# Layer 0's score maxima by half batches, most of them beside the attention that uses them

## The reference, cut to what matters

```python
scores = jnp.einsum('bhqd,bhkd->bhqk', q, k) * scale
scores = jnp.where(causal, scores, -jnp.inf)
y_ar = jnp.einsum('bhqk,bhkd->bhqd', jax.nn.softmax(scores, axis=-1), v)
e = v[:, :, 1:, :] - y_ar[:, :, :-1, :]
...
y_ma = jnp.einsum('bhqk,bhkd->bhqd', ma, e)
```

## Time and profile before

| | us |
|---|---|
| runs | 725.0, 719.17, 721.73 (median 721.73) |
| profiled execution, its own time | 721.84 |
| its span, first to last instruction | 720.0 |
| busy PE, DVE, ACT, POOL | 511.9, 365.3, 196.8, 182.3 |
| reductions of maxima on DVE (L1059), 160 of 690 ns | 110.0 |
| matmuls of maxima without the masks' (L1378, `sb_m_sets`), 160 | 82.5 |
| exps on ACT (L812), 80 of 1,026 ns | 80.3 |
| mean granted TensorE clock | 0.863 |

### The profile page before, as it was taken

How to read it: one execution, slowest core, us unless ns; L and a number is a source line. 1 busy time by engine, 2 the same in 40 slices (tenths; PEclk the granted TensorE clock), 3 DMA queues, 4 the chain that set the end, 5 groups by cost and what they waited for, 6 DMA issues and landing times.

```text
span 720.0 us, 9924 instructions
## 1 busy us (share of the span) xinstructions
PE 511.9 (71%) x3706; PEld 329.5 (46%) x3706; DVE 365.3 (51%) x950; ACT 196.8 (27%) x278; POOL 182.3 (25%) x208
## 2 busy tenths in 40 slices
PE   1755784799899889998878529914778888735930
PEld 1624432344634544453467517802445655524930
DVE  4444745367676856760535431224969677430211
ACT  1342231453245144336234302102223111101200
POOL 8550436001010110111012560045322022031035
PEclk9987887699999999999989958965899999655975
DMA  8434668732442253142070012114743530001213
GB/s 282 185 116 148 210 212 248 177 103 64 92 133 78 79 131 104 53 90 82 1 234 1 30 39 57 45 32 132 203 142 79 160 97 16 1 15 51 60 40 98
DMA packets 61471, 74.16 MB, mean 103 GB/s; under 512 B 6772, under 2 KB 38128, under 8 KB 61168
## 3 DMA queue, kind: packets, MB, share of 16 engines
q1 hardware_dynamic: 59376, 69.34, 33.3%
...
## 4 chain that ended last, share of the span: by engine, by line
PE 47%; DVE 18%; POOL 11%; issue 8%; DMA 6%; ACT 5%; SPq 5%; POOLq 0%; DVEq 0%; ACTq 0%
PE ps_accum L1378 21%; PE ps_pair L1378 16%; PE ps_turn L1378 5%; POOL xe_scr L574 4%; DMA sb_ring<-sb_qs 3%; SPq L358 2%; POOL sb_rstd L558 2%; PE ps_turn L1386 2%; DVE sb_work L1132 2%; POOL sb_work L720 2%; DVE sb_work L1270 1%; DVE sb_mpart L1059 1%; DVE sb_values L969 1%; DVE sb_stats L960 1%; SPq L366 1%
## 5 line engine op out<-in xcount | busy, mean ns | idle before, releaser
L812 ACT ACTIVATE sb_work<-ps_pair 128x1024 f32<-128x1024 f32 x80 | 80.3, 1026 | 51.0 <-PE ps_pair L1378 50.2
L1059 DVE TENSOR_REDUCE sb_mpart<-ps_turn 128x4 f32<-128x512 f32 x80 | 55.0, 687 | 46.6 <-PE ps_turn L1378 46.5
L1378 PE MATMUL ps_pair<-sb_ring,sb_xsets 128*128 128x512 f32 x160 | 64.5, 480 | 15.6 <-DMA sb_ring<-sb_qs 10.1
L1059 DVE TENSOR_REDUCE sb_mpart<-ps_accum 128x4 f32<-128x512 f32 x80 | 55.0, 688 | 20.9 <-PE ps_accum L1378 20.2
L1378 PE MATMUL ps_accum<-sb_work,sb_v_aug 128*32 128x128 f32 (+3 forms) x768 | 58.6, 400 | 0.3 <-ACT sb_work L812 0.3
L1378 PE MATMUL ps_turn<-sb_ring,sb_m_sets 128*128 128x512 f32 x80 | 40.5, 506 | 20.7 <-DMA sb_m_sets<-q_scr 11.0
L1378 PE MATMUL ps_accum<-sb_ring,sb_m_sets 128*128 128x512 f32 x80 | 42.0, 525 | 3.9 <-DVE sb_mpart L1059 3.7
L1378 PEld LDWEIGHTS ps_pair<-sb_ring,sb_xsets 128*128 128x128 f32 x160 | 30.7, 199 | 26.6 <-issue 14.5
L556 POOL TENSOR_SCALAR sb_ve<-sb_mv 128x4 f32<-128x4 f32 x24 | 5.6, 235 | 144.4 <-DVE sb_mv L963 144.0
L624 POOL TENSOR_TENSOR sb_e_pad<-sb_v_next,sb_y_ar 128x128 f32<-128x128 f32 x16 | 7.3, 458 | 127.2 <-DVE sb_y_ar L1102 127.2
L1270 DVE TENSOR_TENSOR sb_work<-ps_pair,sb_cst 128x1024 f32<-128x1024 f32 x32 | 37.5, 1215 | 2.2 <-PE ps_pair L1378 2.2
...
## 6 DMA issues: line engine op xcount, KB each, us to landing
...
```

The costliest lines, as they stand in the source:

```text
L812: act.activation(banks[:, 2 * i:2 * i + 2], pair[u % 2][:], ACT.Exp, scale=SCALE).then_inc(s["exp_done"], 1)
L1059: dve.tensor_reduce(mpart[:, m // NPAIR, m % NPAIR, :], max_banks[m % 2][:].rearrange("p (h k) -> p h k", h=HL), AX.X, ALU.max).then_inc(s ...
L1378: return pe.matmul(dst, lhsT, rhs, start=start, stop=stop, skip_group_check=True)
```

## The change

Maxima are numbered through over all batches (n from 0 to 159), and finished by half batches q (two sets, HALF = 20 units) where they were finished by batches.

- Ahead of attention only batch 0's first 20 units are run: 12 in front 3, none in front 2, eight behind the fronts.
- In attention, batch 0's slot 0 has 20 units (sets 2 and 3 of batch 0 itself), and each slot after it ten: slots 1 to 3 of batch b have the first three sets of batch b+1, slot 0 of batch b+1 its last. So batch 3's slot 0 has ten units, and its other slots none. In slots 1 and 3 a slot's first step has none, and the other four have 3, 2, 3, 2.
- `max_of_tiles`, `max_turn` and `max_t` are done for each half batch: eight times where there were four, once ahead of attention, and then in step u = 5 (half 2b+1) and step u = 15 (half 2b+2) of the first pass. ACT's copy stands behind the exp of that step and behind `answers_out`. `mT` has two tiles of 8 rows. The first unit of a half waits until ACT has copied the half before.
- On SP, set 2 and set 3 of batch 0's maxima are loaded ahead of `keep_features(2)` and `keep_softmax(3)`; `load_exp_set(0, ...)` stands behind `keep_features(3)`; `next_max_set(2)`, which holds until unit 29 has run, stands ahead of `load_state(0)`; a row of maxima is issued right behind its set's loads.

```diff
--- before.py
+++ after.py
@@ -106,6 +106,27 @@
 LAST_OF_UNIT = [EXP_PAIRS[2 * i + 1][0] for i in range(NPAIR // 2)]
 NM, NX, NG_X = NS * NPAIR, NS * NPAIR // 2, NPAIR // 2
 STEPS = NS * NT
+HALF = 2 * NPAIR
+UNITS = B * NS * NPAIR
+
+
+def max_units(b, u):
+    hs, i = u // NG_X, u % NG_X
+    if b == 0 and hs == 0:
+        return HALF + 4 * i, HALF + 4 * i + 2, HALF + 4 * i + 4
+    first = NPAIR * (NS * b + NS - 1 + hs)
+    if first >= UNITS:
+        return UNITS, UNITS, UNITS
+    at = (0, 0, 3, 5, 8, 10) if hs % 2 else (0, 2, 4, 6, 8, 10)
+    return first + at[i], first + (at[i] + at[i + 1]) // 2, first + at[i + 1]
+
+
+def max_turn_in(b, u):
+    if u == NG_X:
+        return 2 * b + 1
+    if u == 3 * NG_X and b + 1 < B:
+        return 2 * b + 2
+    return None
 
 def build(nc, x_in, bias_cols, w_attn_t, w_k2_t, w_proj_t, b_proj, w1_t, w2_t, b2,
...
@@ -387,18 +408,16 @@
                     hold(sp, s["v_aug"], b)
                 sp.dma_start(values_of[b % 2][:], v_scr[b].rearrange("(t p) d -> p t d", p=P)).then_inc(s["v_in"], 16)
-            def next_max_set(b, hs):
-
-                hold(sp, s["smax_mm"], NM * b + NPAIR * (hs + 1))
-                if hs + 2 < NS:
-                    load_max_set(b, hs + 2)
-                elif b + 1 < B:
-                    load_max_set(b + 1, hs + 2 - NS)
+            def next_max_set(n):
+
+                hold(sp, s["smax_mm"], NPAIR * (n + 1))
+                if n + 2 < B * NS:
+                    load_max_set((n + 2) // NS, (n + 2) % NS)
             def max_row(b, hs):
                 sp.dma_start(ring[3 * HD:3 * HD + 1, hs % 2].bitcast(F32),
-                             mT[HL * hs:HL * hs + HL].bitcast(F32)).then_inc(s[f"xset{hs % 2}"], 16)
+                             mT[hs // 2][HL * (hs % 2):HL * (hs % 2) + HL].bitcast(F32)).then_inc(s[f"xset{hs % 2}"], 16)
             def keep_values(b):
@@ -433,45 +452,42 @@
             keep_values(2)
             keep_softmax(1)
             keep_features(1)
-            next_max_set(0, 0)
             keep_values(3)
-            next_max_set(0, 1)
             keep_softmax(2)
+            next_max_set(0)
             keep_features(2)
+            next_max_set(1)
             keep_softmax(3)
+            keep_features(3)
             hold(sp, s["ffn_h"], NF * B)
             for hs in range(2):
                 load_exp_set(0, hs)
-            keep_features(3)
             hold(sp, s["v_kept"], 16 * B)
             load_values(0)
-            for kept in ("q_kept", "k_kept"):
-                hold(sp, s[kept], 48 * B)
-            next_max_set(0, 2)
             hold(sp, s["max_t_evac"], 1)
             for hs in range(2):
                 max_row(0, hs)
-            next_max_set(0, 3)
-            for kept in ("mq_kept", "mk_kept"):
+            for kept in ("q_kept", "k_kept", "mq_kept", "mk_kept"):
                 hold(sp, s[kept], 48 * B)
             hold(sp, s["zeroed"], 7)
             for b in range(B):
+                if b == 0:
+                    next_max_set(2)
                 load_state(b)
                 if b + 1 < B:
                     load_values(b + 1)
                 for hs in range(NS):
-                    if b + 1 < B:
-                        next_max_set(b + 1, hs)
+                    if NS * b + NS - 1 + hs < B * NS:
+                        next_max_set(NS * b + NS - 1 + hs)
                     hold(sp, s["st_mm"], NX * b + NG_X * (hs + 1))
                     if hs + 2 < NS:
                         load_exp_set(b, hs + 2)
+                        hold(sp, s["max_t_evac"], 2 * b + 2)
                         max_row(b, hs + 2)
                     elif b + 1 < B:
                         load_exp_set(b + 1, hs + 2 - NS)
-                if b + 1 < B:
-                    hold(sp, s["max_t_evac"], b + 2)
-                    for hs in range(2):
-                        max_row(b + 1, hs)
+                        hold(sp, s["max_t_evac"], 2 * b + 3)
+                        max_row(b + 1, hs + 2 - NS)
...
@@ -785,15 +801,15 @@
                 if b:
                     features(b - 1)
-            def max_t(b):
-
-                act.wait_ge(s["max_t"], b + 1)
-                if b:
-                    act.wait_ge(s["xset0"], 192 * b)
-                    act.wait_ge(s["xset1"], 192 * b)
+            def max_t(q):
+
+                act.wait_ge(s["max_t"], q + 1)
+                if q >= 2:
+                    act.wait_ge(s["xset0"], 192 * (q // 2))
+                    act.wait_ge(s["xset1"], 192 * (q // 2))
                 else:
                     act.wait_ge(s["q_kept"], 48 * B)
-                act.copy(mT, turn[1][0:H, :]).then_inc(s["max_t_evac"], 1)
+                act.copy(mT[q % 2], turn[1][0:H // 2, :]).then_inc(s["max_t_evac"], 1)
             def answers_out(b, hs):
@@ -812,9 +828,9 @@
                     act.activation(banks[:, 2 * i:2 * i + 2], pair[u % 2][:], ACT.Exp, scale=SCALE).then_inc(s["exp_done"], 1)
                     if hs and i == 0:
                         answers_out(b, hs - 1)
+                    if max_turn_in(b, u) is not None:
+                        max_t(max_turn_in(b, u))
                 answers_out(b, NS - 1)
-                if b + 1 < B:
-                    max_t(b + 1)
                 act.wait_ge(s["yar_mm"], b + 1)
                 act.copy(y_tmp[0][:], turn[1][:]).then_inc(s["yar_evac"], 1)
...
@@ -1106,23 +1124,18 @@
             def attention(b):
-                if b + 1 < B:
-                    at = [6] + [NPAIR * (hs + 1) + 3 for hs in range(NS - 1)] + [NM]
-                    maxima(b + 1, 0, 4)
-                    if b:
+                for u in range(NX):
+                    hs, i = u // NG_X, u % NG_X
+                    first, _, last = max_units(b, u)
+                    maxima(first, last)
+                    if b and u == 1:
                         moments(norm_first(B + b - 1), x[b - 1], (b - 1) % 2)
-                    maxima(b + 1, 4, 6)
-                    if b:
+                    if b and u == 2:
                         normalise(norm_first(B + b - 1), x[b - 1], xn_third[b - 1], (b - 1) % 2)
-                    for hs in range(NS):
-                        maxima(b + 1, at[hs], at[hs + 1])
-                        if hs < NS - 1:
-                            answers_divide(b, hs)
-                    max_of_tiles(b + 1)
-                else:
-                    norm(norm_first(B + b - 1), x[b - 1], xn_third[b - 1])
-                    for hs in range(NS - 1):
-                        answers_divide(b, hs)
+                    if u + 1 < NX and max_turn_in(b, u + 1) is not None:
+                        max_of_tiles(max_turn_in(b, u + 1))
+                    if hs and i == 1:
+                        answers_divide(b, hs - 1)
                 answers_divide(b, NS - 1)
                 for n in range(2 * NT):
@@ -1191,11 +1204,11 @@
                 norm(b, x[b], xn_first[b])
             for b in range(B):
                 before_attention(b)
-            maxima(0, 6 * NT, 7 * NT)
+            maxima(12, 16)
             split(B - 1, 0)
             split(B - 1, 1)
             query_features(B - 1)
-            maxima(0, 7 * NT, NM)
+            maxima(16, HALF)
             max_of_tiles(0)
             for b in range(B):
                 attention(b)
@@ -1466,41 +1479,47 @@
                 last.then_inc(s["ka_t_mm"], 1)
             def before_attention(b):
-                m = 3 * NT * (b - 2)
-                output(b, (lambda i: max_scores(0, m + i, m + i + 1)) if b >= 2 else None)
-                if b + 1 < B:
-                    hidden(b + 1, (lambda i: max_scores(0, m + 4 + i, m + 5 + i)) if b >= 2 else None)
+                last = b == B - 1
+                output(b, (lambda i: max_scores(i, i + 1)) if last else None)
+                if last:
+                    max_scores(4, 8)
                 else:
-                    max_scores(0, m + 4, m + 8)
+                    hidden(b + 1)
                 if b >= 2:
                     turn_keys(b - 2)
                     pe.wait_ge(s["ka_tok"], b - 1)
                 if b:
                     turn_second(b - 1, values_of[(b - 1) % 2])
                     project(b - 1)
-                if b >= 2:
-                    max_scores(0, m + 8, m + 12)
+                if last:
+                    max_scores(8, 12)
                 if b + 2 < B:
                     turn_first(b + 2, xn_first[b + 2])
-            def max_scores(b, first, last_m):
-
-                for m in range(first, last_m):
-                    hs, (qt, kt) = m // NPAIR, MAX_PAIRS[m % NPAIR]
-                    if m % NPAIR == 0:
-                        pe.wait_ge(s[f"mset{hs % 2}"], 80 * (2 * b + hs // 2 + 1))
-                    if b or m >= 2:
-                        pe.wait_ge(s["smax_red"], (NM + NT) * b + m - 1)
-                    dst = max_banks[m % 2][:]
```

(51 more changed lines are left out.)

38 lines of the change are left out of this document (20 added, 18 removed).

## The result

The changed kernel takes 756.13 us (748.42 to 759.77, 4 runs), the one before 721.23 in its company: 1.0442 times as long, 95% interval [1.0343, 1.0541]. The forecast was 742 with a range to 752, so the direction was right and the size was not. The profiled execution is one of 757.92 us with a span of 756.1, so 36.1 us of span are to be found.

The account below looks back on a forecast made before the run. The order of work was taken to bound the kernel as much as PE's amount (47% of the chain). Terms -14.1 + 4.7 + 4 + 20.5 + 1.7 + 3.4 = +20.2 us on 721.84 gave 742 us, range 727 to 752.

Parts of the forecast that it names:

- start of attention: First scores come 14.1 us earlier: front 2 gains 17.3, the stretch behind the fronts loses 3.2.
- units, batch 3's slot 0: Ten units moved into batch 3's slot 0, with the wait for the residual, add 4.7 us.
- units, batch 0's slot 0: Ten more units in batch 0's slot 0, 20 in all, add 4 us.
- seven turns, no falls: Mid-pass turns make PE wait for a 3.7 us chain through ACT's copy and exp; +20.5 us for seven.
- falls of the clock: Idle time at turns drops the clock to 1.2 GHz in one turn of three, 1.44 us each; +3.4 us.
- SP's hold in batch 0: In batch 0's attention, next_max_set(2) holds SP's queue, so PE waits for step 8's row; +1.7 us, bounds 0 and 5.
- the sum that begins "After: 12.5": SP's queue in batch 0's attention: row issued 29.8 to 30.4 us after the first scores, landing about 31.5.
- Rival 1: The clock falls at all seven turns, 1.44 us each or longer; 748.7 us, up to 753; chance 0.12.
- The front: Front 2 loses its 12 units and the 11.0 us wait for their set; gain 17.3 us, bounds 11 and 18.5.
- Rival 2: In attention, turns are mostly hidden, about 1 us each, as PE catches up; 725.1 us; chance 0.11.
- Rival 3: Attention starts 18.5 us earlier, units and turns (0.6 us) cost little, SP's hold nothing; 713.5 us; chance 0.08.
- Rival 4: The set lands late and front 3 waits in place of front 2; gain some 6 us, 750; chance 0.04.

Follow-up runs that it names:

- e3: The changed kernel with eight matmuls that nobody reads added around each turn in the pass, run while PE waits; 743.55 us.
- e2: The changed kernel with ACT copying the turned maxima behind the exp of the step after the turn, not ahead of it; 743.61 us.
- e4: The changed kernel without the seven turns inside the pass, both halves' rows coming from the first turn (not the right maxima); 732.97 us.
- e1: The changed kernel with load_state(0) and load_values(1) ahead of next_max_set(2) in SP's order; 749.73 us.
- e6: The changed kernel with units spread evenly, PE's max_turn a step later, ACT's copy behind that step's exp, load_state(0) ahead of next_max_set(2); 727.3 us.
- e8: The changed kernel without turns inside the pass (not the right maxima), units spread evenly, load_state(0) ahead of next_max_set(2); 719.77 us.

## Why the prediction was wrong, by its own steps

The slots' table gives each term of the prediction's sum a measured one (after less before, by slot).

| term | predicted | measured | |
|---|---|---|---|
| start of attention | -14.1 | -15.9 | 128.49 to 112.57 |
| units, batch 3's slot 0 | +4.7 | +4.7 | 10.0 to 14.7 |
| units, batch 0's slot 0 | +4 | +5.3 | 15.8 to 21.1 |
| seven turns, no falls | +20.5 | +22.5 | slots 1 and 3 of e3 over before: 3 x 2.7, 3 x 4.2, 1.8 |
| falls of the clock | +3.4 | +9.2 | five behind turns, 7.7 (after over e3), the term as it was forecast, and one in batch 3's second pass, 1.5 |
| SP's hold in batch 0 | +1.7 | +7.4 | slot 1: 21.34 against e3's 13.96 in the other batches |
| a wait in batch 1's slot 2 | none | +2.9 | 11.4 to 14.3 |
| sum | +20.2 | +36.1 | |

The slots left out and the part behind attention cancel within 0.1 us.

**The mechanism was right, two of its sizes were not, and a wait was missing.** The step that decided, the turn in the middle of the pass, was right by more than its total: the chain (3.7 us predicted, 3.57 measured at its first turn), where PE would stand idle and for whom, that ACT's order was the reason (e2), and the total at full clock (20.5 against 22.5). That the totals lie so close is in part luck: of the 22.5, e4 shows about 15 to be the turns (slot 1 2.0, slot 3 2.5, batch 3 1.9), and the rest is what the slots without turns still take over before. I had priced that at 0.6 for two units moved; bunched 0, 3, 2, 3, 2 they cost 0.3 to 0.6 in slot 1 and 1.2 in slot 3, and a slot 3 keeps 0.6 more whose cause wasn't tried. Batch 0's slot 1 enters here with the other batches' 2.7, and what it has above them is the next term; the two overlap there, as e4 shows.

**SP's hold in batch 0** is the step that failed most, where the sum that begins "After: 12.5" puts the row: the term was mis-sized, +1.7 against +7.4. The hold ended 14.5 us after the first scores and not 12.5 (likely since the first 9.4 us ran at 1.2 GHz with twice the units: granted 0.50 from 112.57 to 122); the row went 32.5 us after them (29.8 predicted), and took 3.05 us to release PE, not 1.7. The wait of 4.97 us that this gave was at the upper bound of 5 that I had written; what I had left out is that the clock falls around so long a wait (granted 0.73 from 142.5 to 155); the other 2.4 us of the 7.4 are in that stretch. e1 shows that the order, not the amount of the loads, made it, and e6 and e8 that slot 1 is 12.1 to 12.3 once the hold is behind the loads and the turn's wait is gone.

**The clock** was the other: one fall in three turns, by the three second passes of before, against five in seven in the profiled execution. The rows were the wrong neighbours, as the text itself noted when it counted more idle time in a turn. Rival 1, a fall at every turn, was nearer to the truth than the forecast; the price of a fall was right, 1.44 against 1.57. The Trainium skill's "TensorE: Matmul & The Clock Gate" (section "A second HAM failure mode: psum-queue depth-cycling") names this kind of loss, and gives no count; the trace agrees in kind, with five falls. That every turn falls, and the 748.7 with it, was my reading of the page. In e1's profile it is again five of seven, but not the same five, though the idle times are the same to 0.02 us: what decides at a given turn stays open. So does the spread of the runs from 748 to 760. The number of falls would be an easy reason, but e1, with as many falls in its profile, stays within 2.9 us, and the kernel before, which has no turns in the pass, spreads over 10 us and more (718.77 to 729.27 in 16 of 17 runs, the last at 733.98).

**The front** was right and a little too small: 17.3 predicted for front 2, and 19.1 is what output(3)'s start shows (78.09 to 59.02), 1.0 of which was there before front 2 began. Behind the fronts it lost 3.1, as predicted (26.9 us from the start of project(3), the first row above, to the first scores, where the prediction had 27.0).

**The wait in batch 1's slot 2** (2.22 us for a row, and a fall of the clock) is a term that the prediction did not have. It is in after and in e6 (2.37 us) but in none of the other profiled executions. Its row was issued 0.9 us later against the slot's end than before, behind a set's issue of 1.20 us; in e6 it was 1.0 later, behind another slow issue. Why those were slow stays open.

Rival 2 (turns mostly hidden, about 1 us each) falls with e4. Rival 3 (faster) needed turns of 0.6 us, or of 1.8 to break even, and with the units' order they took 3.2 at full clock; its start of attention was 2.6 us too early and its units 4 us too cheap. Rival 4 did not happen: the set was in when output(3) came for it. (The low end of the forecast's own range, 732, is 733 by the terms that it names.)
